# Hadamard transform of the down-projection weights computed inside the cross-attention units

## The reference

```python
up_gate = jnp.einsum('bsd,hd->bsh', x, W1)      # W1, W3: (2048, 512)
up_lin = jnp.einsum('bsd,hd->bsh', x, W3)
hidden = jax.nn.silu(up_gate) * up_lin
hidden = fwht(hidden)                            # Walsh-Hadamard over 2048, scaled 1/sqrt(2048)
out = jnp.einsum('bsh,dh->bsd', hidden, W2)      # W2: (512, 2048)
```

## Time and profile before

| what | value |
|---|---|
| median of 3 runs | 4343.22 us (4336.3 to 4344.09) |
| the profiled execution | 4339.26 us, span 4337.5 us |
| cross-attention | 2930 to 3685.7 us of the span |
| block of `hadamard_weights` | 3685.7 to 3757 us |
| layer norm ln3 | 3757.7 to 3791 us |
| feed-forward | 3791 to 4330 us |

### The profile page before, as it was taken

How to read it: one execution, slowest core, us unless ns; L and a number is a source line. 1 busy time by engine, 2 the same in 40 slices (tenths; PEclk the granted TensorE clock), 3 DMA queues, 4 the chain that set the end, 5 groups by cost and what they waited for, 6 DMA issues and landing times. The chain is left out here.

```text
span 4337.5 us, 75366 instructions
## 1 busy us (share of the span) xinstructions
PE 3928.8 (91%) x26288; PEld 2913.2 (67%) x26288; DVE 2995.1 (69%) x5082; ACT 2443.1 (56%) x4829; POOL 545.4 (13%) x445
## 2 busy tenths in 40 slices
PE   3899999999999999999999999984988988299998
PEld 2677777777777777777777777762444444188887
DVE  3788888887888888878888888864655554722222
ACT  2677667676777676766767677761544445211111
POOL 0000000000000000000000000002333332311110
PEclk7999999999999999999999999996999999699999
DMA  2010111010101110101001010105556552100001
GB/s 76 15 42 27 33 36 33 26 42 16 43 26 33 35 33 26 42 17 43 26 32 37 16 43 26 33 8 85 90 80 96 84 94 35 44 20 20 20 15 39
DMA packets 133895, 171.97 MB, mean 40 GB/s; under 512 B 12508, under 2 KB 79836, under 8 KB 132988
## 3 DMA queue, kind: packets, MB, share of 16 engines
q1 hardware_dynamic: 131068, 165.84, 16.3%
q10 hardware_dynamic: 2432, 1.05, 0.2%
HBM read 142.92 MB, written 21.76 MB: 38 GB/s over the span
## 5 line engine op out<-in xcount | busy, mean ns | idle before, releaser
L407 PE MATMUL pj<-xh,w_hi 128*128 128x512 f32 x1536 | 684.4, 446 | 16.8 <-DVE w_lo L746 16.5
L407 PE MATMUL pj<-xh,w_lo 128*128 128x512 f32 x1536 | 607.8, 396 | 0.0
L407 PE MATMUL pj<-xl,w_hi 128*128 128x512 f32 x1536 | 600.9, 391 | 0.0
L1572 DVE TENSOR_REDUCE row_max<-s 128x1 f32<-128x512 f32 x512 | 342.4, 687 | 272.9 <-PE s L1326 269.7
L1057 POOL TENSOR_TENSOR silu_z<-silu_z,exp_z 128x512 f32<-128x512 f32 x128 | 185.3, 1469 | 2641.1 <-ACT exp_z L633 2641.1
L1506 ACT ACTIVATE probs<-s 128x512 f32<-128x512 f32 x512 | 291.4, 595 | 325.2 <-PE s L1350 319.4
L407 PEld LDWEIGHTS pj<-xh,w_hi 128*128 128x128 f32 x1536 | 291.1, 190 | 65.7 <-DVE w_lo L746 17.0
L407 PEld LDWEIGHTS pj<-xh,w_lo 128*128 128x128 f32 x1536 | 288.8, 188 | 66.2
L407 PEld LDWEIGHTS pj<-xl,w_hi 128*128 128x128 f32 x1536 | 292.2, 190 | 50.2 <-issue 14.8
L1350 PE MATMUL s<-q_stack,k_stack 128*128 128x512 f32 x512 | 249.0, 489 | 75.2 <-DMA q_stack<-row_maxima 67.2
L812 DVE SCALAR_TENSOR_TENSOR conv_v<-conv_in,conv_w_section,conv_v 128x512 f32<-128x512 f32 x384 | 288.0, 750 | 10.7 <-ACT conv_v L616 1.6
(11 more groups left out here) (258 smaller groups left out, 9887.4 us busy)
## 6 DMA issues: line engine op xcount, KB each, us to landing
w_raw<-in_w_in SPq DMA_DIRECT2D x128, 256.0 KB, 6.2
decays<-decay_by_head SPq DMA_DIRECT2D x64, 512.0 KB, 3.8
decays<-decay_by_head SPq DMA_DIRECT2D x64, 256.0 KB, 5.1
q_stack<-qk_parts SPq DMA_DIRECT2D x128, 128.0 KB
k_stack<-qk_parts SPq DMA_DIRECT2D x128, 128.0 KB
f_raw<-in_f_w SPq DMA_DIRECT2D x32, 256.0 KB, 2.6
x_all<-in_x SPq DMA_DIRECT2D x4, 1024.0 KB, 10.3
source<-in_ctx SPq DMA_DIRECT2D x8, 512.0 KB
```

Of the source, the lines that this page charges most:

```text
L407: mm = pe.matmul(pj[j % 2][:, :], a[:, j, k * P:(k + 1) * P], b[:, k, bp * WIN:(bp + 1) * WIN], start=(n == 0), stop=(n == 3 * KT - 1))
L1572: dve.reduce_max(mx[g % 2][:, i:i + 1], s1[n % 2][:, :], AX_X).then_inc(E["rm"].sem, 1)
```

## The change: what it does, and the diff

`hadamard_weights` is gone. W2 is laid out on the host in 16 slices of 32 of its 512 columns, one per unit; a slice holds 16 chunks x 32 columns, [128, 512]. In unit u, TensorE multiplies the slice with `had` behind step 15 (`pe_down_weights`, into bank `pb`), ScalarE copies it with the scale behind the exponential of step 16, and GpSimd does the four levels as 8 operations of 128 x 256 and the split into `had_hi` and `had_lo`. SyncE loads the slice of unit u+2 and stores the two parts of unit u, 256 KB each, to DRAM (`down_parts`). During ln3, SyncE reads the parts of groups 0 and 1 back (4 DMAs of 1 MB, runs of 512 bytes), and those of groups 2 and 3 at the start of the feed-forward. `wd_hi` and `wd_lo` are now ordered [unit, chunk, column], so the moving operand of `pe_down` is 16 runs of 32 elements, 2 KB apart. `pe_down` waits for its group, and TensorE's loop over the middle groups is unrolled.

```diff
-def layernorm_transposed(nc, tag, x_all, cols, xh, xl, load=None):
+def layernorm_transposed(nc, tag, x_all, cols, xh, xl, prefetch=None):
...
+            def load_down(u):
+                if u > 1:
+                    E["hp"].wait(sp, u - 2, 0)
+                sp.dma_start(h_raw[u % 2][:, :], a["f_w2"][:, u, :]).then_inc(E[f"hw{u % 2}"].sem, 16)
+
+            def store_down(u):
+                E["hlo"].wait(sp, u, 0)
+                for i, part in enumerate((h_hi, h_lo)):
+                    sp.dma_start(down_parts[i, :, u, :], part[:, :].bitcast(F32)).then_inc(E["hst"].sem, 16)
...
+                sp.dma_start(had[:, :], a["consts"][:, 2 * P:3 * P]).then_inc(loaded, 16)
+                for u in range(2):
+                    load_down(u)
...
                     if f and b + 2 < BATCH:
                         load_mask(b + 2)
+                if u < UNITS - 2:
+                    load_down(u + 2)
+                store_down(u)
+            E["hst"].wait(sp, UNITS - 1, 31)
...
+        def pe_down_weights(pe, u, b, f, has1, has2):
+            if is_first(u):
+                pe.wait_ge(loaded, 16 * 9)
+            if has2:
+                E["full"].wait(pe, u + 2, 1)
+            elif has1:
+                E["vsb"].wait(pe, u + 1, 0)
+            else:
+                E["hc"].wait(pe, u - 1, 0)
+            E[f"hw{f}"].wait(pe, b, 15)
+            pe.matmul(pb[:, :], had[:, :], h_raw[f][:, :], start=True, stop=True).then_inc(E["hp"].sem, 1)
...
+                if n == 15:
+                    pe_down_weights(pe, u, b, f, has1, has2)
...
-                    if n == 18 and has2:
-                        E["full"].wait(pe, u + 2, 1)
-                    elif n == 18 and has1:
-                        E["vsb"].wait(pe, u + 1, 0)
+                    if n == 18:
+                        E["hc"].wait(pe, u, 0)
                     pe_spread(pe, u - 1, n - 18)
...
+        def act_down_weights(act, u):
+            E["hp"].wait(act, u, 0)
+            E["hlo"].wait_before(act, u)
+            act.activation(h_buf[0][:, :], pb[:, :], ACT.Copy, scale=float(np.float32(1 / np.sqrt(FH))))\
+               .then_inc(E["hc"].sem, 1)
...
+        def pool_down_weights(pool, u):
+
+            E["hc"].wait(pool, u, 0)
+            for lv in range(4):
...
+                for i in range(2):
+                    pool.tensor_tensor(dst_[:, :, i, :], src_[:, :, 0, :], src_[:, :, 1, :],
+                                       (ALU.add, ALU.subtract)[i]).then_inc(E["hb"].sem, 1)
+            E["hb"].wait(pool, u, 7)
+            E["hst"].wait_before(pool, u)
+            pool.tensor_copy(h_hi[:, :], h_buf[0][:, :]).then_inc(E["hhi"].sem, 1)
+            E["hhi"].wait(pool, u, 0)
+            pool.tensor_tensor(h_lo[:, :], h_buf[0][:, :], h_hi[:, :].bitcast(F32), ALU.subtract)\
+                .then_inc(E["hlo"].sem, 1)
...
+                pool_down_weights(pool, u)
                 if u:
                     pool_final(pool, u - 1)
...
-def hadamard_weights(nc, a, wd_hi, wd_lo):
...
+            for g in range(2, GROUPS):
+                load_down(sp, g)
             with sp.Fori(1, GROUPS) as g:
                 load(g, False)
...
-                                   q[:, bass.ds(g * FG + c, 1), :].rearrange("p a b -> p (a b)"),
+                                   p[c % 2][:, t * P:(t + 1) * P], q[:, :, g * FG + c, :],
...
+            def load_down(sp, g):
+                for i, part in enumerate((wd_hi, wd_lo)):
+                    sp.dma_start(part[:, :, g * FG:(g + 1) * FG, :].bitcast(F32),
+                                 down_parts[i].rearrange("p u (c j) -> p u c j", j=HC)[:, :, g * FG:(g + 1) * FG, :])\
+                        .then_inc(wd_in[g].sem, 16)
```

More of the change, by code:

```diff
@@ L31 @@
 SS_SCALE = 2.0 ** 20
+FH = 2048
+FC = FH // P
+HC = HID // (2 * BATCH)
 class Section:
@@ L105, in layernorm_transposed @@
         block = ctx.enter_context(nc.Block())
-        n_loads = 0 if load is None else load(None, None)
-        if load is not None:
+        if prefetch is not None:
             @block.sync
             def _(sp):
-                load(sp, loaded)
+                prefetch(sp)
         @block.vector
         def _(dve):
-            if n_loads:
-                dve.wait_ge(loaded, 16 * n_loads)
             with dve.Fori(0, TILES) as i:
@@ L1171, in cross_attention @@
         rt = m.sb("recip_masked", [P, 4, HH, XD])
+        had = m.sb("had", [P, P])
+        h_raw = [m.sb(f"had_raw{i}", [P, FC * HC]) for i in range(2)]
+        h_buf = [m.sb(f"had_buf{i}", [P, FC * HC]) for i in range(2)]
+        h_hi, h_lo = (m.sb(n, [P, FC * HC], F32R) for n in ("had_hi", "had_lo"))
         parts_d = nc.dram_tensor("qk_parts", [2, 2, 2, P, HID], F32).ap()
@@ L1506, in act_unit @@
                 act.activation(pt[:, n % RP, :], s2[n % 2][:, :], ACT.Exp).then_inc(E["ex"].sem, 1)
+                if n == 16:
+                    act_down_weights(act, u)
                 if n in (11, 14) and has2:
@@ L1683, in pool_recip @@
                                mcol[:, u // 2, :].unsqueeze(2).unsqueeze(3).to_broadcast([P, 4, HH, XD]), ALU.mult)                .then_inc(E["rt"].sem, 1)
+        def pool_down_weights(pool, u):
+            E["hc"].wait(pool, u, 0)
+            for lv in range(4):
+                src_, dst_ = (h_buf[i][:, :].rearrange("p (a two r) -> p a two r", two=2, r=HC << lv)
+                              for i in (lv % 2, 1 - lv % 2))
+                if lv:
+                    E["hb"].wait(pool, u, 2 * lv - 1)
+                for i in range(2):
[7 more added lines that the diff above has]
+                .then_inc(E["hlo"].sem, 1)
         def pool_final(pool, u):
@@ L1868, in pe_down @@
             if c == 0:
+                wd_in[g].wait(pe, 0, 31)
                 E["out"].wait_before(pe, r)
@@ L1892, in _ @@
             pe_up(pe, 0, 0, 0, 0)
-            group(0, False)
-            with pe.Fori(1, GROUPS - 1) as g:
-                group(g, False)
-            group(GROUPS - 1, True)
+            for g in range(GROUPS):
+                group(g, g == GROUPS - 1)
         @block.scalar
@@ L2008, in build, with prefetch @@
                       beta, decay_rows)
-        cross_attention(nc, y_all, cols, a)
+        down_parts = nc.dram_tensor("down_parts", [2, P, 2 * BATCH, FC * HC], F32).ap()
+        cross_attention(nc, y_all, cols, a, down_parts)
         with ExitStack() as ffn:
             mf = Memory(nc, ffn)
-            wd_hi = mf.sb("wd_hi", [P, FC, HID], F32R)
-            wd_lo = mf.sb("wd_lo", [P, FC, HID], F32R)
-            hadamard_weights(nc, a, wd_hi, wd_lo)
+            wd_hi = mf.sb("wd_hi", [P, 2 * BATCH, FC, HC], F32R)
+            wd_lo = mf.sb("wd_lo", [P, 2 * BATCH, FC, HC], F32R)
+            wd_in = [mf.event(f"wd_in{g}", 32) for g in range(FC // FG)]
+            def load_down(sp, g):
[3 more added lines that the diff above has]
+                        .then_inc(wd_in[g].sem, 16)
+            def prefetch(sp):
+                for g in range(2):
+                    load_down(sp, g)
             xh = mf.sb("fxh", [P, KT, TOK], F32R)
```

79 lines of the change are left out of this document (10 added, 69 removed).

## The result

| kernel | median | runs |
|---|---|---|
| before, beside the changed kernel | 4340.64 us | 4336.3 to 4344.09 |
| changed | 4284.68 us | 4281.75 to 4289.4 |

The ratio is 0.9873, with an interval of 0.9856 to 0.989: the change takes off 56 us, and the forecast of 4288 was 3.3 us high. The same kernel measured once more, beside the later experiments, gave 4283.39 us (ratio 0.9866, 0.9849 to 0.9882). The profiled execution took 4285.89 us, its span is 4284.1; the one before has 4337.5, so 53.4 us are to be found between the two traces.

What follows compares the result with a forecast made beforehand. TensorE, busy for 91% of the span, was taken as the bound, so only its idle stretches could be gained. 4339.3 - 70.7 + 8 + 10 = 4286.6, stated as 4288 with a share of the 4 us to the median; range 4270 to 4312.

Steps and rivals of the forecast that it cites:

- The gain of 70.7 us: Hadamard block before ln3: removing its 71.96 us, less one remaining change of block of 1.22, gains 70.7 us.
- The product and the copy, +8: Cross-attention units: TensorE's product and ScalarE's copy, partly taken up by gaps, cost 0.5 us a unit: +8, 0 to 21.
- The rival in which gaps take both up: Cross-attention: gaps hide product and copy, the engines' turns spare the read-back of the maxima; 4269 to 4275 us, chance 0.15.
- SyncE's queue, +10: Unit ends in cross-attention: added load and stores lengthen the queue ahead of the maxima's read-back: +10 us, 0 to 23.
- The stacks that the store's wait holds back: Even units' ends: odd heads' stacks queue behind the stores, no longer beside the read-back; may give a little back, unsized.
- The rule of the Trainium skill: Maxima's read-back: its semaphore waits for all earlier writes of that DMA engine, so the full 20 us; 4297, chance 0.25.
- Reading back, 0 and at most 4: Ln3: reading 4 MB of parts back fits into its 33.3 us; cost 0, at most 4 us.
- The strided operand, 0: Feed-forward, pe_down's 768 matmuls: a moving operand in runs of 32 costs 0 us.
- costs a little: Feed-forward: the operand in runs costs a little or the start is late; 4 to 18 us more, 4291 to 4306, chance 0.05.
- What the profile after would show: Signs expected in the later trace's unit lengths, read-back waits, GpSimd's slice, ln3's DMA share and f_acc, with 1 to 2 us longer units.

Runs made afterwards that it cites:

- the variant of the kernel before: The kernel before with only wd_hi and wd_lo laid out so that pe_down's operand is in runs of 32: 4352.02 us, against 4343.28.
- the staged mask: Changed kernel with slice load and stores behind the stacks, plus mask_prep loaded early into its own tile and copied by VectorE: 4248.42 us, ratio 0.9789.

## Why the prediction was right, point by point

- *The gain of 70.7 us.* Right: 71.3. The change of block took 0.65 us instead of 1.22.
- *The product and the copy, +8.* Mis-sized: 0, by the run without them. The step that counted 0.5 us a unit on a TensorE busy for 92% took its busy time for path. The product takes 0.46 us from its start to the next scores' in 15 of the 16 units and not 0.70, and what it pushes back is made good by fewer waits for exponentials: 131 and 69.8 us after, 150 and 78.9 before, and 151 and 79.7 in the run without product and copy. The rival in which gaps take both up was right on this point.
- *SyncE's queue, +10.* Right that the read-back pays for traffic, wrong on how. I priced it by length (2.1 us an odd end, 0.7 an even one). The odd ends, already full with `mask_prep` and the stacks, paid nothing (5.5 to 6.0, then 5.2 to 5.7; over all traces with the same cross-attention 5.2 to 6.2 and 4.9 to 5.8). Even ends paid some tenths. The one end that had a gap, unit 13's, paid 3.7 us of wait and 5.4 of unit, and nothing in the forecast named it: the earlier trace rows show one even and one odd end, and I took them for all. The rest of the 7: the other units +4.5 in sum, and the stretch up to the first wait -3.0. That wait fell from 11.56 (10.01 in the variant of the kernel before) to 8.86 and is 8.5 to 9.4 in all variants of the changed kernel; the cause stays open.
- *The stacks that the store's wait holds back.* The forecast named this, as "may give a little back". Where the load of a slice stands beside the read-back, the hold is worth 17 us, which a kernel showed that has the load but not the hold. Without that load the same early stacks cost nothing (the kernel before, even ends of 2.3 to 3.0 us), so what the hold gives back is a cost that the load itself would have brought.
- *The rule of the Trainium skill* (DMA: Bandwidth & Descriptors, Queues, rings and completion order), by which the wait would take up every earlier write. As the sum that I made of it, 8 us at odd ends, it fell: they didn't move with 2.1 us more or less ahead. What the traces show are two levels, 2.0 to 3.1 us with gaps and 4.8 to 7.4 with full engines, and 16 waits of 196 between them. The rule may still have a part in the second; no run here takes it apart from the turns of the engines.
- *Reading back, 0 and at most 4.* +1.0 from `f_raw` to `f_gate`. Ln3 itself was 2.2 shorter; its 16 statistics took 9.59 us instead of 11.58, and I haven't tried why.
- *The strided operand, 0.* This is the step that failed: it costs 8.7 us in `f_acc` and some 11 in the feed-forward. "For run lengths that differ by level the median is 193 ns" was read from float16 operands of 64 columns, and carried to float32r ones of 512. The Trainium skill's page SBUF — State Buffer (Door 1) gave 0 too; the trace doesn't agree, with 251.3 against 240.0 ns for runs of 128 bytes. The rival "costs a little" had 4 to 18 us and 0.05, too little for an operand that no row tested.
- *What the profile after would show.* Units longer by 1 to 2 us: the eleven from the third on by 0.2 on average. Odd ends 6 to 8: no, 5.2 to 5.7. Even ends 2 to 3: nearly. `f_acc` as long as `f_gate`: no. GpSimd's slice in 7 to 8: 8.0, as its operations of 128 x 256 took 0.73 us and not 0.61. A DMA share of nearly 1 for 11 to 15 us at the start of ln3: 1.2 at 290 GB/s from 3698 to 3710, and 0.03 after it.

So 4288 held 18 us for cross-attention, of which 7 were there (3 to 8 over the traces), and nothing for the feed-forward, which took 11. Two errors of 11 us cancelled, and that the number fits to 3.3 us is luck. A sum that fits doesn't prove its terms.

## What to carry to other kernels

A small transfer on which an engine waits should be issued into a gap of the DMA engines: here the wait was mostly 2.0 to 3.1 us through a gap and 5 to 7 through full engines, a loss of clock came with it, and moving one 256 KB load out of the way in six units brought 30 us (27 in the second trace). Ask of every DMA, and of every wait in its queue, what it keeps away from such a transfer: a store that seemed to be cost held back transfers that, beside the load, cost more. And an operand's form that no row of the trace has is an unknown with a price on both sides; lay it out as one run, or in runs of 64 and more, where that is free.

## What the hardware showed that I had not expected

- A moving float32r operand of 512 columns in runs of 32 elements takes 250 to 251 ns instead of 240, of 16 elements 256, of 8 and 4 elements 246 and 243 (the last hardly clear of the 2 ns that the place in the group makes), of 2 elements 474, of 64 nothing more; the distance of the runs (256, 512, 2048 bytes) makes no difference of over 1 ns.
- The wait for an 8 KB read-back has two levels, 2.0 to 3.1 us and 4.8 to 7.4, with 16 of 196 waits between them, and 786 kB more in front of it do not lengthen the upper one.
- A wait of TensorE costs more than its length: over 4.7 us it came with a loss of 3.4 us of full speed in 75 of 76 cases, at 2.0 to 3.1 us mostly with 1.7, and with nothing in 13 of 104. By the time of the eight scores behind it, 9 of the 30 us that the staged mask gained were this.
